# A fused two-layer graph network on one core: rows brought to four partitions by a wider block transpose and written to memory by one transfer

## The reference, cut to what matters

```python
def _gat(inp, adj_mask, W, a):
    h = jnp.matmul(inp, W)
    f1 = jnp.matmul(h, a[:F_, 0]);  f2 = jnp.matmul(h, a[F_:, 0])
    e = jax.nn.leaky_relu(f1[:, :, None] + f2[:, None, :], 0.2)
    if adj_mask is not None:
        e = jnp.where(adj_mask[None, :, :] > 0, e, NEG_INF)
    att = jax.nn.softmax(e, axis=2)
    return jax.nn.elu(jnp.einsum('bij,bjf->bif', att, h))

# block 1: h = relu(layernorm(x))
out = relu(h @ mlp1_w + mlp1_b); residual = out        # 128 -> 256 features
out = _gat(relu(out), None, W_fc, a_fc)                # attention 1, 256 wide, no mask
out = elu(out) + residual
out = relu(out @ mlp2_w + mlp2_b); residual = out      # 256 -> 128
out = _gat(relu(out), adj, W_hand, a_hand)             # attention 2, 128 wide, masked
x = x + relu(elu(out) + residual)
# block 2: h = relu(layernorm(x)); attention 3, 128 wide, masked
x = x + elu(softmax(mask(leaky_relu(s1 + s2))) @ (h @ W))
```

## Time and profile before

| | |
|---|---|
| median of three runs | 433.07 us (432.94 to 433.32) |
| span of the profiled execution | 429.0 us |
| around the span (median less span) | 4.1 us |
| TensorE (PE) busy | 411.1 us, 96% |
| VectorE (DVE) busy | 357.8 us, 83% |
| ScalarE (ACT) busy | 315.7 us, 74% |
| GpSimd (POOL) busy | 24.9 us, 6% |
| small writes of rows and moments | 144 and 52 transfers |

### The profile page before, as it was taken

How to read it: one execution, slowest core, us unless ns; L and a number is a source line. 1 busy time by engine, 2 the same in 40 slices (tenths; PEclk the granted TensorE clock), 3 DMA queues, 4 the chain that set the end, 5 groups by cost and what they waited for, 6 DMA issues and landing times.

```text
span 429.0 us, 8704 instructions
## 1 busy us (share of the span) xinstructions
PE 411.1 (96%) x2544; PEld 352.7 (82%) x2544; DVE 357.8 (83%) x1226; ACT 315.7 (74%) x764; POOL 24.9 (6%) x53
## 2 busy tenths in 40 slices
PE   6999999999999999999999999999999999989782
PEld 4688779887898899797998788989879799869772
DVE  7786588878998898988898868979698899889974
ACT  2655659658796787786878688687867887799774
POOL 0000000000001000010100000100000000000000
PEclk9999999999999999999999999999999999999997
DMA  7854323123423142232222213222320122120001
GB/s 209 278 146 130 105 74 121 74 76 98 125 98 75 53 138 84 52 101 74 75 82 68 75 53 98 79 72 74 80 87 10 49 93 59 45 80 24 27 1 57
DMA packets 39461, 36.42 MB, mean 85 GB/s; under 512 B 4080, under 2 KB 30320, under 8 KB 39408
## 3 DMA queue, kind: packets, MB, share of 16 engines
q1 hardware_dynamic: 37408, 33.17, 26.1%
q10 hardware_dynamic: 2000, 2.63, 1.8%
HBM read 31.46 MB, written 4.32 MB: 83 GB/s over the span
## 4 chain that ended last, share of the span: by engine, by line
PE 87%; DVE 5%; ACT 3%; issue 2%; DMA 1%; SPq 0%; POOL 0%; ACTq 0%; DVEq 0%
PE bank L1530 24%; PE bank L1437 23%; PE bank L1426 13%; PE bank L1416 6%; PE bank L1477 6%; PE bank L1455 6%; PE bank L1445 3%; PE bank L1538 2%; PE bank L1496 1%; PE bank L1466 1%; DMA row<-row_scratch 1%; DVE stats L1036 1%; DVE u L1265 1%; ACT ext L826 1%; ACT e L911 1%
## 5 line engine op out<-in xcount | busy, mean ns | idle before, releaser
L1530 PEld LDWEIGHTS bank<-ext,prob 128*128 128x128 f32 x1024 | 119.6, 192 | 6.3 <-issue 4.9
L1530 PE MATMUL bank<-ext,prob 128*128 128x129 f32 x1024 | 122.1, 275 | 0.3 <-DVE prob L1207 0.2
L1437 PE MATMUL bank<-ext,prob 128*128 128x257 f32 x512 | 119.0, 380 | 0.0
L1437 PEld LDWEIGHTS bank<-ext,prob 128*128 128x128 f32 x512 | 94.8, 190 | 17.3 <-issue 4.5
L1211 DVE SCALAR_TENSOR_TENSOR prob<-prob,square,mask_t 128x512 f32<-128x512 f32 x98 | 70.6, 739 | 0.9 <-ACT prob L859 0.8
L1426 PE MATMUL bank<-wfc_sb,o_t 128*128 128x259 f32 x256 | 64.0, 382 | 0.4 <-ACT o_t L790 0.4
L859 ACT ACTIVATE prob<-row,square 128x512 f32<-128x512 f32 x78 | 54.1, 720 | 0.1
L1426 PEld LDWEIGHTS bank<-wfc_sb,o_t 128*128 128x128 f32 x256 | 46.3, 190 | 9.6 <-issue 4.5
L903 ACT ACTIVATE y<-bank,recip 128x128 f32<-128x128 f32 x128 | 39.3, 369 | 15.3 <-DVE recip L1257 14.2
L911 ACT ACTIVATE e<-y,minus_one 128x512 f32<-128x512 f32 (+1 forms) x70 | 47.7, 688 | 1.4
L1265 DVE SCALAR_TENSOR_TENSOR u<-e,y 128x512 f32<-128x512 f32 (+1 forms) x70 | 44.1, 638 | 4.2 <-issue 2.2
(11 more groups left out here) (98 smaller groups left out, 499.1 us busy)
## 6 DMA issues: line engine op xcount, KB each, us to landing
row<-row_scratch SPq DMA_DIRECT2D x36, 256.0 KB, 3.3
moments_row<-moments_scratch SPq DMA_DIRECT2D x13, 512.0 KB, 3.8
x_in<-in_x SPq DMA_DIRECT2D x16, 256.0 KB, 5.3
x_res<-in_x SPq DMA_DIRECT2D x16, 256.0 KB, 4.6
out<-y_out SPq DMA_DIRECT2D x15, 256.0 KB, 3.9
normed<-in_x_t SPq DMA_DIRECT2D x14, 256.0 KB, 4.3
row_scratch<-square_t SPq DMA_DIRECT2D x144, 0.5 KB
adj_sb<-in_adj ACTq DMA_DIRECT2D x1, 1024.0 KB, 8.1
```

The lines of the kernel that those rows point to most:

```text
L1437: last = nc.tensor.matmul(filled[:, 0:H + 1], gat1.targets(b, t, c), gat1.features_and_one(b, t), start=(t == 0), stop=(t == C - 1))
L1530: last = nc.tensor.matmul(filled[:, e * (D + 3):e * (D + 3) + D + 1], L.targets(b, t, c), L.features_and_one(b, t), start=(t == 0), stop=( ...
```

## The change

**The wider transpose.** `square`, `square_t`, `moments_n` and `moments_t` grow from 128 x 32 to 128 x 128 numbers a slot, and tile c of a vector now stands at the first column of its own 32 x 32 block. After the block transpose, vector k of tile c lies on partition 32 j + k at columns 32 c to 32 c + 31, for j from 0 to 3. So the row lies on the four partitions 0, 32, 64 and 96. The zeroing memsets at lines 961 and 980 grow from 64 to 256 numbers for each partition.

**Fewer transfers.** A row is written with one transfer of 4 x 4 x 32 numbers in place of four of 4 x 32. The moments are written with two (one for the means, one for the roots) in place of four. The same bytes go to the same places in memory, and the loads that follow are unchanged.

**The adjacency matrix** lands in layer 3's second weight tile (`gat3.prob[:, 1]`), and the tile `adj_sb` goes away. The slower program loads it again before it uses it, and its scratch space `lrelu` moves onto `moments_row`.

```diff
-        adj_sb = sb("adj_sb", [P, C, N], i32)
...
-        moments_n = sb("moments_n", [P, 2, 32])
-        moments_t = sb("moments_t", [P, 2, 32])
+        moments_n = sb("moments_n", [P, 2, C * 32])
+        moments_t = sb("moments_t", [P, 2, C * 32])
...
-        meanvar = [moments_n[:, :, 0:2 * C].rearrange("p s (c m) -> p s c m", c=C), meanvar2]
+        meanvar = [moments_n[:].rearrange("p s (c r) -> p s c r", c=C)[:, :, :, 0:2], meanvar2]
...
-                self.square = sb(f"square{k}", [P, 2, 32])
-                self.buv = self.square[:, :, 0:3 * C].rearrange("p s (k c) -> p s k c", k=3)
-                self.square_t = sb(f"square_t{k}", [P, 2, 32])
+                self.square = sb(f"square{k}", [P, 2, C * 32])
+                self.buv = self.square[:].rearrange("p s (c r) -> p s r c", c=C)[:, :, 0:3]
+                self.square_t = sb(f"square_t{k}", [P, 2, C * 32])
...
+        adj_sb = gat3.prob[:, 1].bitcast(i32)
...
-        lrelu = adj_sb[:, 0:2].bitcast(fp32)
+        lrelu = moments_row[:].rearrange("p s c m i -> p s (c m i)")[:, :, 0:N]
...
-        moments_written = slots("moments_written", TURNED + SPREAD, ROWS)
+        moments_written = slots("moments_written", TURNED + SPREAD, 2)
...
-                self.row_written = slots(f"row_written{k}", ROW_BY_TENSOR[k], ROWS)
+                self.row_written = slots(f"row_written{k}", ROW_BY_TENSOR[k])
...
-                rows = moments_scratch[b.slot].rearrange("(m k i) -> k m i", m=2 * C, k=ROWS)
-                for k in range(ROWS):
-                    sp.dma_start(rows[k], moments_t[32 * k:32 * k + 2 * C, b.slot]).then_inc(
+                rows = moments_scratch[b.slot].rearrange("(c m k i) -> m k c i", c=C, m=2, k=ROWS)
+                for m in range(2):
+                    sp.dma_start(rows[m], moments_t[m:P:32, b.slot].rearrange("k (c i) -> k c i", c=C)).then_inc(
                         moments_written.sem(b), 16)
...
-                rows = L.scratch[b.slot].rearrange("(c k i) -> k c i", c=C, k=ROWS)
-                for k in range(ROWS):
-                    sp.dma_start(rows[k], L.square_t[32 * k:32 * k + C, b.slot]).then_inc(s.row_written.sem(b), 16)
+                sp.dma_start(L.scratch[b.slot].rearrange("(c k i) -> k c i", c=C, k=ROWS),
+                             L.square_t[0:P:32, b.slot].rearrange("k (c i) -> k c i", c=C)).then_inc(
+                    s.row_written.sem(b), 16)
```

More of the change, by code:

```diff
@@ L706, in store @@
                 sp.dma_start(out_v[b.n][:, rest], y_out[:, b.slot, rest]).then_inc(stored.sem(b), 16)
+            if general:
+                sp.dma_start(adj_sb[:], adj.rearrange("(c p) j -> p c j", c=C)).then_inc(s_adj, 16)
             return {
@@ L1019, in bounds @@
             def bounds():
+                dve.wait_ge(s_adj, 32)
                 nc.vector.tensor_scalar(bound[:], adj_sb[:], 0.0, 1e38, ALU.is_gt, ALU.mult).then_inc(s_mask, 1)
```

## The result

The changed kernel takes 434.78 us (median of 6 executions, 432.03 to 435.08) beside 433.00 us for the kernel before on the same chip (6 executions, 431.13 to 433.39). The ratio is 1.005, with a 95% interval of 1.0027 to 1.0074, which lies wholly above 1: the kernel is slower by about 0.5%. The forecast was 433.7 us and no change. Its range (432.8 to 434.8) just holds the time, but "no change", which it gave as likeliest, is wrong.

What follows compares the result with a forecast made beforehand. VectorE bounds the start, TensorE the rest until about 379 us. 429.0 + 0.64 (memsets) + 0.03 (transposes) = 429.7 us of span, plus 4.1 around it: 433.7 us, no change; range 432.8 to 434.8.

Steps and rivals of the forecast that it cites:

- The bound: VectorE sets the start, TensorE has no gap from 9.31 to about 379 us; a loss at the start moves everything.
- Part 1: Four wider memsets on VectorE at the start, 0.16 us more each, all on the path: +0.64 us.
- The first matmul: TensorE's first real matmul, at 9.31 us before, was to start at 9.95 us, later by the memsets' 0.64 us.
- rival A: Gap in TensorE's warming at 5.5 us delays the clock's rise, first matmuls at half speed: 434.7 us; chance 0.13.
- 4.1 us around the span: The 433.07 us time less the profiled 429.0 us span, added unchanged to the new span of 429.7 us.
- Part 2: 49 wider transposes on VectorE, 0.10 us more each, 4.8 us in all, mostly hidden: 0.03 us in the sum.
- the named place: Normed tiles near 197 us, read by TensorE 0.06 us after they are done; TensorE would be 0.04 us late.
- the handful: At most a handful of small-margin places where transposes delay TensorE: 0.03 us in the sum, up to 0.3 in the range.
- Rival B: Transposes cost VectorE 7.6 us more and a tenth reaches TensorE, 0.76 us: 434.4 us; chance 0.14.
- Part 3: 134 fewer write issues on SP, each row's load 0.7 to 0.9 us earlier, off the path: 0 us.
- Rival C: In the tail everything waits for the row landing at 375.99; 0.8 us come back: 432.9 us; chance 0.13.
- Part 4: The adjacency matrix's transfer lands in another tile, first used much later, with no wait added: 0 us.

Runs made afterwards that it cites:

- e2: The kernel before with only the four memsets at the start widened to 256 numbers; median 432.72 us, ratio 1.0025.
- e4: The kernel before with four warming transposes on TensorE in place of seven; median 432.99 us, ratio 1.0024.
- h2: The same kernel as e2, run again in another group; median 433.30 us, ratio 1.0024.
- f4: The kernel before, TensorE warmed from 0.99 us with ten matmuls on a GpSimd-zeroed tile in place of the transposes; median 431.07 us, ratio 0.9984.
- f3: The changed kernel with wide memsets on GpSimd and TensorE warmed from 0.99 us by ten matmuls on a zeroed tile; median 431.51 us, ratio 0.9997.
- g3: The kernel before with only the wide memsets, TensorE warmed from 0.99 us by twelve matmuls on a zeroed tile; median 432.17 us, ratio 1.0010.
- g4: The changed kernel with TensorE warmed from 0.99 us by twelve matmuls on a zeroed tile, nothing else; median 432.75 us, ratio 1.0027.
- g2: f3 with each row and the moments written by four transfers again, the wide transposes kept; median 434.20 us, ratio 1.0059.
- e3: The whole changed kernel with the four wide memsets moved from VectorE to GpSimd; median 431.93 us, ratio 1.0006.
- e1: The changed kernel with ten warming transposes on TensorE in place of seven; median 432.99 us, ratio 1.0021.
- h3: f4 with the four narrow memsets of the kernel before moved to GpSimd; median 431.38 us, ratio 0.9994.

## Why the prediction was wrong

**The bound (right).** TensorE has no gap in the middle and VectorE sets the start, so what is lost at the start moves everything: e2 shows it in the purest form, +0.80 us from 5.3 us on.

**Part 1 (right in kind, mis-sized).** The term was +0.64 us; it measured +0.80 to 0.81 in the traces. The duration is 0.27 us, as said, 0.16 more than the 0.11 of the earlier trace rows, which is what my slope had. But each widened memset moves what comes behind it by 0.20 us: TensorE's warming starts 0.20 us later behind the first (3.81 for 3.61), the statistics 0.81 us later behind all four. A slope from two short rows, with starts printed to 0.01 us, was a fifth low; as printed, 0.06 us for 64 numbers is 0.94 ns a number and not 0.83, which would have given 0.72 us. The sentence from the Trainium skill (VectorE: DVE Perf Modes, "Zero memsets can be issued as uint32"), one cycle for each element whatever the type, gave an estimate of 0.80 us with the same page's 0.96 GHz. The trace's 0.81 us agrees with it.

**The first matmul (the step that failed).** The prediction says "First matmul then: 9.95. Sum: +0.64 us." It came at 10.59, with the first four matmul instructions at 3.32 us and no wait ahead, and by 14 us TensorE was 2.61 us behind and not 0.64. The step took TensorE's pace after the start for given. This was rival A, seen in the right place (a gap on TensorE at 5.5 us) and with about the right time (434.7 us), but with a chance of 0.13. The argument that held it down was that TensorE now has more time before its real work. In the changed kernel this extra time didn't help: 21 of 22 executions are late. Elsewhere it may have: e4 has the gap without it and is late twelve times of twelve, while e2 and h2, with the gap and the extra time, are late 13 times of 24. A break in the warming work stands in all of these kernels; in e4 and the changed one it went with a late clock nearly every time, in e2 no more often than in the kernel before (63 of 128).

**Not seen at all: before's own two groups.** Half of the executions of the kernel before already lose this. By their times the three runs shown at first were all late ones, while the profiled execution, with its full-pace matmuls at 9.31 and a span of 429.0 us, was an early one. (Its own time isn't on record; with the 1.8 us below it would be 430.8.) The "4.1 us around the span" was a sign of it: in the profiled executions of the experiments time and span differ by 1.7 to 1.9 us. The prediction added up 429.0 + 4.1 and so carried about 2 us of late clock along as if it were launch overhead.

**The sum, with what the runs measured.** Memsets 0.8 (by the trace), the middle 0.4 (0.37 from f4 to f3, 0.48 from g3 to g4, by means), and late executions always in place of half the time 1.0 (e4 to before, 433.03 to 432.00, by means) give 2.2 us. The 22 executions of the changed kernel have a mean of 434.22 us, 2.2 above the 432.0 of before. The parts and the whole agree within their errors of some 0.2 us each.

**Part 2 (right in kind, too small in the sum).** 306 and 311 ns (0.30 forecast), hidden for the most part; the named place lost 0.05 us (0.04 forecast). But there are five such steps, and the largest, which adds up to 0.23 us by 155 us, wasn't foreseen; the transpose of the moments stands at 152.16 ahead of the weights that TensorE takes then. It is 0.49 us in all against 0.03 in the sum: the handful was right, and its size was not, even against the 0.3 us allowed in the range. Rival B's mechanism is real and cost 0.49 us where it was given 0.76.

**Part 3 (right in the sum, off in the price).** 0 us, as said. An issue of a 4 x 4 x 32 pattern takes 0.53 us, above the upper bound of 0.45, so the load is 0.5 us and not 0.7 to 0.9 us sooner. Rival C is out: the wait before the last batch is 1.68 us as before, and the chain of the changed kernel doesn't pass through a row any more. g2 adds what the prediction missed: once a row lies in blocks, writing it with four transfers would cost 2.7 us, so the merged write isn't a gain but the condition of the new layout.

**Part 4 (nothing shown for the change, but its transfer is not free of waits).** The adjacency matrix lands 6.2 to 9.2 us after its issue in the 17 traces, with no clear difference between the two layouts. VectorE waits up to 1.22 us for it, in the new layout as in the old:

```profile
19.88 2.29 DVE L1003 TENSOR_REDUCE has_edge<-adj_sb 128x4 f32<-128x2048 int32 x1 [0.15 <-DMA adj_sb<-in_adj]
```
```profile
21.75 2.29 DVE L1005 TENSOR_REDUCE has_edge<-adj_sb 128x4 f32<-128x2048 int32 x1 [1.22 <-DMA adj_sb<-in_adj]
```

The first is the kernel before, the second h2. In f4, where it waits 0.67 us, TensorE loses 0.29 us near 24 us, and in h2 0.84 us. In the traces with a late clock there is no such wait; there the matrix has landed before VectorE comes to it. So the time within a group has a second source of spread beside the clock.

**What stays open.** e2 and the changed kernel have the same start on TensorE to 0.01 us, gap included. Yet the 24 executions of e2 and h2 split in two, while only 1 of 22 of the changed kernel was early. The memsets' gap can't be all of it. e3 and e1, which keep the layout, the transposes and the merged writes, split too, so none of these alone makes the clock late. It may take the gap and something of the rest together; no run takes the rest apart. Nor does any run take the gap and the amount of warming work apart: e4 has three transposes fewer, e1 three more, and the early warming starts sooner, lasts longer and multiplies zeros, all at once. What makes the clock rise early in one execution and late in the next of the same kernel isn't visible in a trace.

## What to carry to other kernels

Before you count a delay at the start of a kernel bound by TensorE, look whether it opens a gap in TensorE's warm-up. Of the three kernels with such a gap here two were late nearly always, and the late clock cost more than the delay (1.0 beside 0.8 us). Warm from an idle engine's zeroed tile and not from a constant that the busiest engine builds. Put wide memsets on an idle engine and not on the one that sets the start (e3; for the narrow ones h3 showed no gain). And compare the profiled execution's own time with the runs: where the two don't fit (4.1 us around a span that is 1.8 us elsewhere), the profile and the median are of different executions.

## What the runs showed of the hardware that was not expected

- The times of the kernel before fall into two groups about 1.7 us apart (0.4%) on the same chip. In the 17 traces the record of the granted clock is up at 3.9 to 8.2 us with full-pace first matmuls, or at 13.0 to 15.5 us.
- In the kernels with ten or more warming transposes or matmuls some executions have a mean granted clock of 0.989 to 0.991 and are 0.9 to 2.0 us slower than the mean of the rest of their run.
- The same transfer of 1 MB took 6.2 to 9.2 us to land.
- The warming work may be transposes: in the trace before, TensorE had run nothing else when the clock rose at 7.41 us.
- The price of issuing a small transfer hangs on its pattern more than on its bytes: 0.29 us for 4 x 32, 0.53 for 4 x 4 x 32, and 0.55 for 1 x 4 x 32.
- A second transpose straight behind the first takes 269 in place of 306 ns, and three memsets of 256 numbers on GpSimd take 0.81 us (the one before them 0.31 us), about as long as on VectorE (0.27 us each).
